# Cross-attention in two layers: scores stored negated and scaled with a running minimum, and a one-tensor LayerNorm shift

## The reference

```python
q = einsum('bte,ef->btf', emb, Wq) + bq
k = einsum('bml,le->bme', latent, Wk) + bk
v = einsum('bml,le->bme', latent, Wv) + bv
w = softmax(einsum('bte,bme->btm', q, k) / sqrt(512), axis=1)   # over t
pred = einsum('btm,bme->bte', w, v)
x = pred + emb
y = (x - mean) * rsqrt(var + 1e-6) * gamma + beta                # over e
```

## Time and profile before

| | |
|---|---|
| median of 3 runs | 1253.51 us (1252.52 to 1253.87) |
| span of the profiled execution | 1250.4 us |
| between that span and the median of the runs | 3.1 us |
| TensorE (PE) busy | 1105.8 us, 88% |
| VectorE (DVE) busy | 1121.0 us, 90% |
| ScalarE (ACT) busy | 782.9 us, 63% |
| GpSimd (POOL) busy | 826.7 us, 66% |
| granted TensorE clock, mean | 0.974 |
| HBM traffic | 59.7 MB, 48 GB/s |

### The profile page before, as it was taken

How to read it: one execution, slowest core, us unless ns; L and a number is a source line. 1 busy time by engine, 2 the same in 40 slices (tenths; PEclk the granted TensorE clock), 3 DMA queues, 4 the chain that set the end, 5 groups by cost and what they waited for, 6 DMA issues and landing times.

```text
span 1250.4 us, 26510 instructions
## 1 busy us (share of the span) xinstructions
PE 1105.8 (88%) x8392; PEld 994.2 (80%) x8392; DVE 1121.0 (90%) x2689; ACT 782.9 (63%) x2033; POOL 826.7 (66%) x646
## 2 busy tenths in 40 slices
PE   7989988899988899998899898899899889989874
PEld 7888877788877888887788887788888778888763
DVE  3589999999999999999999999999999999999985
ACT  2466666666576566667666657656666766765743
POOL 0246667767667777766776776777776677677674
PEclk9989999999999999999999999999999999999996
DMA  8101111101111110111110111111011111011000
GB/s 205 69 32 41 55 55 55 44 18 47 54 54 54 54 32 22 54 54 54 54 43 22 43 54 54 54 54 32 22 54 54 54 54 46 21 41 55 15 17 29
DMA packets 19217, 60.14 MB, mean 48 GB/s; under 512 B 4064, under 2 KB 6112, under 8 KB 19184
## 3 DMA queue, kind: packets, MB, share of 16 engines
q1 hardware_dynamic: 16544, 59.71, 14.5%
q10 hardware_dynamic: 2640, 0.01, 0.2%
HBM read 45.03 MB, written 14.68 MB: 48 GB/s over the span
## 4 chain that ended last, share of the span: by engine, by line
DVE 49%; PE 21%; issue 17%; ACT 8%; POOL 2%; DMA 1%; DVEq 1%; ACTq 0%; SPq 0%; POOLq 0%
DVE pr_lo L1016 8%; DVE neg_max L1002 8%; DVE dot_junk L968 6%; ACT probs L782 6%; DVE scores L994 4%; DVE bn L1057 4%; DVE xT_lo L947 3%; DVE nmr L1078 3%; PE oq_bank L554 3%; DVE y L1041 3%; DVE y L1051 2%; PE oq_bank L555 2%; PE oq_bank L556 2%; DVE cT_lo L939 2%; PE pv_bank L623 2%
## 5 line engine op out<-in xcount | busy, mean ns | idle before, releaser
L1234 POOL TENSOR_TENSOR rstd<-ve,minus_half 112x1 f32<-112x1 f32 x128 | 122.1, 954 | 208.8 <-DVE ve L1071 208.8
L782 ACT ACTIVATE probs<-scores,neg_max 125x224 f32<-125x224 f32 x384 | 180.3, 472 | 102.9 <-DVE neg_max L1002 102.0
L594 PE MATMUL oq_bank<-pr_hi,cn_hi 125*128 125x224 f32 x768 | 215.5, 281 | 29.0 <-DVE pr_lo L1016 28.5
L577 PE MATMUL score_bank<-qT_hi,cT_hi 128*125 128x224 f32 x768 | 219.8, 286 | 24.0 <-DVE smax L994 15.7
L825 ACT ACTIVATE z<-y,nmr,rstd 112x512 f32<-112x512 f32 x128 | 104.5, 817 | 186.7 <-DVE nmr L1078 186.7
L596 PE MATMUL oq_bank<-pr_hi,cn_lo 125*128 125x224 f32 x768 | 212.4, 277 | 0.0
L595 PE MATMUL oq_bank<-pr_lo,cn_hi 125*128 125x224 f32 x768 | 212.1, 276 | 0.0
L578 PE MATMUL score_bank<-qT_lo,cT_hi 128*125 128x224 f32 x768 | 208.9, 272 | 0.0
L579 PE MATMUL score_bank<-qT_hi,cT_lo 128*125 128x224 f32 x768 | 208.7, 272 | 0.0
L1212 POOL TENSOR_TENSOR cn_lo<-raw,cn_hi 125x768 fp32r<-125x768 f32 x64 | 131.6, 2057 | 108.5 <-ACT cn_hi L739 60.1
L594 PEld LDWEIGHTS oq_bank<-pr_hi,cn_hi 125*128 125x128 f32 x768 | 148.8, 194 | 36.3 <-issue 36.3
(11 more groups left out here) (106 smaller groups left out, 3235.7 us busy)
## 6 DMA issues: line engine op xcount, KB each, us to landing
raw<-in_ctx_dram SPq DMA_DIRECT2D x32, 750.0 KB
x<-in_x_dram SPq DMA_DIRECT2D x32, 448.0 KB, 4.8
out_dram<-y_out SPq DMA_DIRECT2D x31, 448.0 KB, 3.3
y<-in_L_xattn_Wq_dram SPq DMA_DIRECT2D x4, 512.0 KB, 10.6
x<-in_L_xattn_Wk_dram SPq DMA_DIRECT2D x2, 512.0 KB, 10.0
x<-in_L_xattn_Wv_dram SPq DMA_DIRECT2D x2, 512.0 KB, 11.4
bv_row<-in_L_xattn_bv_dram SPq DMA_DIRECT2D x2, 256.0 KB, 7.2
gamma_row<-in_L_xattn_gamma_dram SPq DMA_DIRECT2D x2, 256.0 KB, 8.0
```

The costliest lines, as they stand in the source:

```text
L577: nc.tensor.matmul(o, hi, qT_hi[:, l, :], start=(l == 0), stop=False)
L594: nc.tensor.matmul(o, hi, pr_hi[0:MP, u.par, c, :], start=(c == 0), stop=False)
L782: ins = act.activation(probs[0:MP, u.par, c, :], scores[0:MP, c, :], ACT.Exp, bias=neg_max[0:MP, c:c + 1], scale=SCALE, accum_out=ssum[0:M ...
```

## The change

The score pass multiplies its sum by -SCALE and keeps a minimum, written to neg_max itself; the negation of the maximum, its semaphore and the buffer smax are gone; exps wait for smax_done of the third or the sixth chunk and use scale -1. The instruction of shift takes the mean as its one tensor, rstd as a per-partition scalar and -1 as a constant, where rstd was a second tensor. Some blank lines ahead of the imports go as well.

```diff
@@
-        smax = sb("smax", [P, MC])
@@
-        neg_max_done = sem("neg_max_done")
@@ exps
-                act.wait_ge(neg_max_done, u.n(m=2, add=half - 1))
+                act.wait_ge(smax_done, u.n(m=6, add=HALF * (half + 1) - 6))
...
                     ins = act.activation(probs[0:MP, u.par, c, :], scores[0:MP, c, :], ACT.Exp,
-                                         bias=neg_max[0:MP, c:c + 1], scale=SCALE, accum_out=ssum[0:MP, c:c + 1])
+                                         bias=neg_max[0:MP, c:c + 1], scale=-1.0, accum_out=ssum[0:MP, c:c + 1])
@@ score_max
-                dve.tensor_tensor_reduce(scores[0:MP, c, :], b[0:MP, (c % 2) * T:(c % 2 + 1) * T], d_row[0:MP, :], 1.0,
-                                         -3.4e38, ALU.add, ALU.max, smax[0:MP, c:c + 1]).then_inc(smax_done, 1)
-
-            def negate_max(u, half):
-                if not u.real:
-                    return
-                cols = slice(HALF * half, HALF * (half + 1))
-                dve.wait_ge(smax_done, u.n(m=6, add=HALF * (half + 1) - 6))
-                dve.tensor_scalar(neg_max[0:MP, cols], smax[0:MP, cols], -SCALE, None, ALU.mult).then_inc(neg_max_done, 1)
+                dve.tensor_tensor_reduce(scores[0:MP, c, :], b[0:MP, (c % 2) * T:(c % 2 + 1) * T], d_row[0:MP, :], -SCALE,
+                                         3.4e38, ALU.add, ALU.min, neg_max[0:MP, c:c + 1]).then_inc(smax_done, 1)
@@ shift
-                dve.scalar_tensor_tensor(out=nmr[0:TP, u.par, h:h + 1], in0=mv[0:TP, u.par, h, 0:1], scalar=-1.0,
-                                         in1=rstd[0:TP, u.par, h:h + 1], op0=ALU.mult, op1=ALU.mult).then_inc(nmr_done, 1)
+                dve.tensor_scalar(nmr[0:TP, u.par, h:h + 1], mv[0:TP, u.par, h, 0:1], rstd[0:TP, u.par, h:h + 1], -1.0,
+                                  ALU.mult, ALU.mult).then_inc(nmr_done, 1)
@@ VectorE's slot
-                    negate_max(now, 0)
...
-                    negate_max(now, 1)
...
-                    negate_max(nxt, 0)
...
-                    negate_max(now, 1)
```

## The result

The changed kernel takes 1181.85 us (median of 4 runs, 1179.99 to 1184.12) against 1253.52 us for the kernel before: a ratio of 0.9434, 95% interval 0.9420 to 0.9448. It is 71.7 us faster. The forecast was 1220.5 us, 33 us faster, with a range down to 1188. The sign was right, the size was less than half, and the time lies outside the range. The profiled execution took 1183.54 us with a span of 1181.7 us.

What follows compares the result with a forecast made beforehand. VectorE, 90% busy, was taken as the bound through port waits for POOL, TensorE close behind; 0.98 - 0.2 + 0.3 = 1.08 us a period by 30.5 periods, 33 us, gave 1220.5 us; own range 1205 to 1238, widened to 1188 to 1243.

Steps and rivals of the forecast that it cites:

- I take 0.3: Odd slot: gain of 0.3 us a period, chosen between 0.6 at best and nothing at worst.
- the loss of 0.2 on POOL: End of even slot: pr_lo delays POOL's chain by 0.85 us, the sum regains 0.62; on balance 0.2 lost.
- Rival A: nmr still waits for the port, so the middle's 0.98 us are lost: 15 us gained, 1238 us; chance 0.12.
- D: Slower: the score pass in its new form takes longer, up to 0.28 us each; 1280 us, chance 0.05.
- C: POOL's chain at the even slot's end swallows the gain, the period stays: 1252 us, chance 0.07.
- start of the even slot: nmr's wait for POOL's sum goes, but pr_lo waits in its place: gain nothing.
- middle of the even slot: Without neg_max ahead of it, nmr starts 0.98 us earlier, and this goes on to the slot's second half.
- the second neg_max: Middle of even slot: its 1.28 us cost nothing, as ScalarE is in the first three exps until then.
- The 1.08 us of the second dot: Odd slot: with earlier exps the second dot finds the port free, 0.74 us instead of 1.82.
- a meeting of the second product and the residual: Odd slot: POOL's earlier L1251 meets the residual y, which puts it back by about 0.5 us.
- rival B: Waits scatter and TensorE becomes the bound: 1137 us at most, more likely half way, 1165 to 1190; chance 0.14.
- what is late next: VectorE's wait for POOL's rstd becomes its largest, 1 to 2 us idle, with oT_lo and TensorE's pv product queued behind.

Runs made afterwards that it cites:

- b_ones: Kernel before, keeping maximum and negation, with each negation split into three one-number instructions and nmr in its new form: 1188.30 us.
- d_mid3: Changed kernel plus one unused instruction over three numbers per partition at the old negation's place in the middle of the even slot: 1218.61 us.
- p_negmax: Only the scores and neg_max part of the change, nmr with two tensors as in the kernel before: 1220.52 us.
- n_start: Changed kernel with nmr as a two-tensor instruction again at the start of the even slot only: 1187.73 us.
- r_rstd_in: Changed kernel with POOL's second rstd of the even slot moved between the second and third sums of probabilities: 1142.95 us.
- n_end: Changed kernel with nmr as a two-tensor instruction again at the end of the even slot only: 1190.91 us.
- r_beta: Changed kernel with POOL's second-half add of beta of the even slot moved ahead of the first rstd: 1214.83 us.
- r_rstd: Changed kernel with POOL's second rstd of the even slot moved ahead of the three sums of probabilities: 1202.47 us.

## Why the prediction was wrong

In short: what the waits were, and where a period loses them, was right. Two terms of the sum were mis-sized: "I take 0.3" for the odd slot, where 1.2 us were measured, and the loss of 0.2 on POOL at the end of the even slot, where 0.18 were gained.

**Right: what kind of time it was.** neg_max and nmr were waits for POOL. b_ones keeps the work and loses the waits, d_mid3 puts back one wait and no work that is used. The new nmr takes 0.2 us however POOL stands. The Trainium skill ("VectorE: DVE Perf Modes", section "Mode 2×_2P") asks of the two-port mode that the outermost dimension that isn't one be even, or equal for source and destination. The rows agree, at the same place: three numbers, as many in as out, take 1.06 us and wait; three instructions of one number, where no dimension is over one, take 0.27 in all and don't. Rivals A and D fell with that: nmr never waits, the score pass is at 381 ns. C fell too. Rival A's case exists as a run, p_negmax, in which nmr does wait: 1220.5 us, where A had 1238. That this is the forecast's own figure is chance; A's price was short by some 17 us too.

**Right: start of the even slot.** Forecast nothing; 0.06 us, pr_lo waits instead, and n_start gives the same from the other side.

**Right, nearly: middle of the even slot.** Forecast 0.98; nmr comes 1.04 us earlier, the exps 0.97, and the fourth exp 1.10, so the second neg_max, counted at nothing, did cost 0.13. All of the 1.1 reaches the second half: cn_lo there starts 10.31 us behind the sum instead of 11.42. d_mid3 confirms the larger part of it from the other side (0.9 to 1.0).

**Wrong: POOL's series at the end of the even slot.** Forecast a loss of 0.2. The order changed as forecast, but pr_lo puts cn_lo back by 0.64, not by its whole 0.85, and that and the sum's saving of 0.61 cancel. And in the old kernel rstd also waited for its ve, which VectorE brought late behind the neg_max (25.66 us behind the period's start, rstd 25.88, though the last sum of probabilities had ended at 25.72). In the new one ve is done 3.4 us before rstd starts. From the add of beta to the product with gamma it is 7.33 us now and was 7.51: a gain of 0.18.

**Wrong, and the larger error: "I take 0.3" in the odd slot.** From POOL's product with gamma to the end of the period it was 10.5 us and is 9.3: 1.2 us. The 1.08 us of the second dot came off whole. What I had set against it, a meeting of the second product and the residual at a cost of 0.5, costs 0.07. Counted from the sum, the exps are 4.1 us earlier and not 3, for I had left out the 1.0 that nmr itself waited ahead of pr_lo; z and the second product are 2.8 us earlier. But the residual, which I had left at its old place, is 1.5 us earlier too, and the two meet only in their ends: the product ends at 645.76, the residual starts at 645.50. In p_negmax, where z is 0.5 later against the first product, the residual pays 0.42 and the slot gains 0.7, close to the estimate of 0.6 at best. And the first dot ends 0.2 us sooner behind the first product than before, since nmr and the two cT_lo ahead of it are done. The upper bound I had given (0.6) was no bound: the 0.5 had been taken off it, from a meeting that I had placed by a hand schedule.

The sum by places: 1.1 + 0.18 + 1.2 = 2.5 us a period, where 0.98 - 0.2 + 0.3 had been set. Times 30 that is 75 us, less 7 us for the dips of the clock.

**Half right: rival B.** The time lies in its half-way band of 1165 to 1190 us, but not for its reason. TensorE doesn't bind the period at full clock (32.0 of 34.4 us busy, and 33.2 can be had); it takes part only in the dips. What it gave VectorE to do, 36.85 - 6.3 = 30.6, was reckoned from the whole period; from VectorE's busy 34.51 it is 28.2, and 28.84 were measured. Its chance of 0.14 was too low chiefly because I trusted a hand schedule of one period to 0.3 us.

**Right, nearly: what is late next.** nmr waits for rstd in the odd slot (46.4 us in all; oT_lo's wait for ScalarE's oT_hi, 55.7 before and 53.1 now, is still larger), the dot behind it for POOL, oT_lo and TensorE's product behind that; r_rstd_in takes 39 us more off by moving that rstd.

## What to carry to other kernels

When two engines share a port, read a tiny instruction with a large mean duration as a wait, look up on the other engine's timeline what it ends with, and ask at each place who needs the port next: a wait of 1.0 to 1.3 us was worth under 0.1, 0.45 or 1.0 us a period here, by place. A one-number-per-partition form didn't wait at all, so splitting an instruction in three can be the cheaper form. When such waits go, the order on the other engine is due for review at once, by trying it: of three reorderings one gained 3.3% and two lost 1.7 and 2.8%.

## What the runs showed of the hardware that wasn't expected

Who gets the port next isn't simply the one that has waited. pr_lo, issued 0.60 us into cn_lo, got it ahead of POOL's next sum, and again in n_end at 0.61 us; issued 0.88 us into cn_lo in r_beta, it was passed over by that sum and took 3.25 us where 0.85 is its time undisturbed. But in the changed kernel pr_lo is issued 0.89 us into the add of beta (668.97 and 668.08) and does get it ahead of cn_lo, so the distance alone doesn't decide. Why isn't settled; no run varied one thing alone.

The dips of the granted clock. In stretches of 4 us around the odd slot of the changed kernel: a period without a dip, then the one of 719.11, then the 4 us ahead of the dip in the next period; and last the same place in r_rstd_in:

```profile
639.84:643.84 4.00, 2.21 (x18) 1.74 (x17) 2.74 (x7) 3.11 (x10) 3.89 (x4) 1.00 0.00 0
...
743.00:747.00 4.00, 2.12 (x17) 1.70 (x16) 2.63 (x7) 3.02 (x10) 3.78 (x4) 1.00 0.00 0
747.00:751.00 4.00, 4.00 (x19) 3.37 (x18) 3.96 (x7) 1.33 (x2) 3.12 (x3) 0.57 0.00 0
...
777.40:781.40 4.00, 2.75 (x25) 2.35 (x23) 2.44 (x5) 3.11 (x11) 3.77 (x6) 1.00 0.00 0
```

```profile
551.00:555.00 4.00, 3.12 (x28) 2.87 (x27) 3.08 (x10) 2.69 (x10) 3.92 (x5) 1.00 0.00 0
```

A dip is some 3.4 us at half of the full clock (0.57 in the mean of 4 us), 1.2 GHz in place of 2.4, in or right behind the place where TensorE waits in the odd slot, for the last sum and then for oT_lo. Ahead of the first of two neighbouring dips it was busy 2.1 of 4 us, ahead of the second 2.75. 19 matmuls are done in the next 4 us, where the period without a dip does 29. That idle place is the one that the late rstd makes. r_rstd_in shortens it (3.12 us busy) and shows no longer period at all. But the same idle place stands in every period of the changed kernel, and only eight of 30 have a dip; n_end has it too (2.64 us busy from 575 to 579) and has no dip between its first and its last period. Why those isn't settled, nor was TensorE's idle time varied by itself. The spacing differs by kernel: two periods in six in the changed kernel, every second in d_mid3. What a dip costs differs as well: nothing at the period of 36.9 us, 1.1 us in the changed kernel where it starts 28.2 us behind the sum, 0.7 where it starts at 26.8, and 0.2 in r_rstd, where it starts at 26.4.
